# A four-layer kernel on one core: head 0's rows sent from the projection, wide exponentials in the last head, and identity products in layer 3's search

## The reference, cut to what matters

```python
# layer 0, attention: 16 heads of 8, all 2048 tokens
scores = norm * jnp.einsum('hbqk,hbnk->hbqn', Q, K)
attn = jax.nn.softmax(scores, axis=-1)
heads = jnp.einsum('hbqn,hbnv->hbqv', attn, V)
...
# layer 3, feed-forward: 8 experts, each takes its 256 best tokens of those left
for e in range(E):
    s = jnp.where(taken, -jnp.inf, scores[:, e])
    _, idx = jax.lax.top_k(s, C)
    parts.append(idx)
    taken = taken.at[idx].set(True)
...
h = jax.nn.gelu(jnp.einsum('ecd,edf->ecf', h, w1) + b1[:, None, :])
h = jnp.einsum('ecf,efd->ecd', h, w2) + b2[:, None, :]
```

## Time and profile before

| what | value |
|---|---|
| median of 3 runs | 1740.68 us |
| lowest and highest run | 1740.24 and 1742.91 us |
| the profiled execution, its own time | 1742.6 us |
| its span, first to last instruction | 1740.8 us |
| mean granted TensorE clock | 0.806 |
| TensorE, VectorE, ScalarE, GpSimd busy | 72, 75, 51, 14% of the span |

### The profile page before, as it was taken

One profiled execution on the slowest core, in us unless ns is written; L12 is line 12 of the kernel. 1 busy time (PEld: TensorE's weight loads), 2 busy tenths in 40 slices (PEclk: granted clock), 3 DMA queues, 4 the chain that ended last, 5 costly groups with the idle time before them and its releaser, 6 DMA issues. The chain is left out here.

```text
span 1740.8 us, 29844 instructions
## 1 busy us (share of the span) xinstructions
PE 1251.1 (72%) x10670; PEld 619.5 (36%) x10674; DVE 1303.1 (75%) x3511; ACT 894.3 (51%) x1789; POOL 237.7 (14%) x279
## 2 busy tenths in 40 slices
PE   6799999999999998475994463060205989833776
PEld 3122222222222223254983342040104556622444
DVE  4999999999999971537237336979898469568783
ACT  4089999999999998322421122020001675512453
POOL 3000000000000000003510314030001321100223
PEclk9589999999999999567995586565656898965668
DMA  2101100001100000000004331000001721022001
GB/s 66 43 3 27 29 21 21 20 23 28 28 22 21 20 3 2 15 29 1 1 1 174 109 84 48 0 0 1 1 1 26 209 69 47 16 93 70 22 22 31
DMA packets 45095, 62.88 MB, mean 36 GB/s; under 512 B 12849, under 2 KB 34420, under 8 KB 44548
## 3 DMA queue, kind: packets, MB, share of 16 engines
q1 hardware_dynamic: 38115, 49.45, 9.6%
q0 software_dynamic: 5568, 10.81, 2.5%
q10 hardware_dynamic: 1264, 0.72, 0.2%
HBM read 34.10 MB, written 13.63 MB: 27 GB/s over the span
## 5 line engine op out<-in xcount | busy, mean ns | idle before, releaser
L822 ACT ACTIVATE l0att_probs<-l0att_ps_sv 128x512 f32<-128x512 f32 x1024 | 555.7, 596 | 84.0 <-PE l0att_ps_sv L792 71.9
L859 DVE TENSOR_REDUCE l0att_half_negmax<-l0att_ps_m 128x1 f32<-128x1024 f32 x480 | 547.2, 1215 | 6.0 <-PE l0att_ps_m L731 6.0
L761 PE MATMUL l0att_ps_sv<-l0att_probs,l_V_aug 128*32 128x256 f32 x4096 | 331.1, 392 | 5.3 <-ACT l0att_pv_sb L813 5.3
L792 PE MATMUL l0att_ps_sv<-l_Q,l_K 51*128 51x512 bf16 x1024 | 200.7, 388 | 2.5 <-ACT l0att_probs L822 0.2
L731 PE MATMUL l0att_ps_m<-l_K,l_Q 48*128 48x512 bf16 x960 | 186.0, 385 | 11.1 <-DVE l0att_half_negmax L859 7.1
L761 PEld LDWEIGHTS l0att_ps_sv<-l0att_probs,l_V_aug 128*32 128x32 f32 x4096 | 83.2, 108 | 199.1 <-issue 104.4
L792 PEld LDWEIGHTS l0att_ps_sv<-l_Q,l_K 51*128 51x128 bf16 x1024 | 49.5, 92 | 216.7 <-ACT l0att_probs L822 204.1
L472 POOL CAST l0att_nm<-l0att_negmax 128x16 bf16<-128x16 f32 x16 | 3.1, 196 | 513.3 <-DVE l0att_negmax L835 513.3
L2826 ACT ACTIVATE l3loc_probs<-l3loc_ps_s 128x320 f32<-128x320 f32 x128 | 48.8, 435 | 37.3 <-PE l3loc_ps_s L2803 36.7
L2004 DVE SCALAR_TENSOR_TENSOR l2spk_lif_v<-l2spk_U 128x64 f32<-128x64 f32 (+1 forms) x368 | 60.4, 205 | 0.0
L2269 PE MATMUL l2spk_ps<-l_X,l2spk_w_terms 128*128 128x512 bf16 x48 | 13.0, 441 | 62.3 <-DVE l_X L2299 62.3
(11 more groups left out here) (734 smaller groups left out, 2358.0 us busy)
## 6 DMA issues: line engine op xcount, KB each, us to landing
l_Q<-l_qp SPq DMA_DIRECT2D x188, 32.0 KB
l_K<-l_kp SPq DMA_DIRECT2D x188, 32.0 KB
l1ffn_W<-in_l_expert_w_dram SPq DMA_DIRECT2D x1, 4096.0 KB
l3f_experts_l_w<-in_l_w_dram SPq DMA_DIRECT2D x2, 2048.0 KB
l_sorted_in<-l1ffn_zeros SPq DMA_DIRECT2D x1, 3072.0 KB
l1exp_rows<-l_sorted_in SPq DMA_DIRECT2D x6, 512.0 KB, 5.4
l_sorted_out<-l1exp_y SPq DMA_DIRECT2D x6, 512.0 KB
l_Q<-in_local_mask_q_dram POOLq DMA_DIRECT2D x2, 1170.0 KB, 18.8
```

The source lines that it names most:

```text
L761: mm = pe.matmul(ps_v[32 * c:32 * c + 32, cols], V_aug[:, kt, h, :], probs[:, kt % 2, c, cols], start=(kt == 0 and part == 0), stop=(kt == ...
L792: pe.matmul(ps_s[:, (n + i) % 3, :], K[at, h % HEAD_BUFS, c1(kt)], Q[at, h % HEAD_BUFS, c4(2 * pair + i)], start=True, stop=True).then_inc ...
L822: act.activation(probs[:, kt % 2, c, :], ps_s[:, n % 3, :], ACT.Exp).then_inc(expd, 1)
L859: dve.tensor_reduce(half_negmax[:, h % 2, t, half:half + 1], src, AX_X, ALU.max, negate=True).then_inc(m_read, 1)
```

## The change

1. The projection of layer 0 gets a callback. SyncE waits there for each part of K and then of Q and issues head 0's 12 low-half transfers as the parts come; the attention block no longer issues them, and TensorE there waits for one semaphore that they all raise.
2. In head 15 the scores of two banks are taken by one exponential of 1,024 columns. The first pair of a key tile goes into a half of `ps_m`, the second into the first two banks of `ps_sv`. Both parts of the value products stand behind the second pair; behind the first pair stands nothing.
3. In the search the digit is added to the result one round later, behind the sum and ahead of the candidates' step (in the half's last round also, with a wait), and for the last digit at the old place.
4. Behind the count and the beside work of rounds 1 to 7 TensorE multiplies the identity up to four times into `ps_t`: four times less two where places are due (rounds 2 to 5 from search 1 on), less two where an expert's up or down products are due (rounds 1 to 5 and 7 from search 2 on).

```diff
+                if rows_of_part is not None:
+                    for m, which in enumerate((1, 0)):
+                        read = NC4 * (m + 1)
+                        sp.wait_ge(high_read, read)
+                        rows_of_part(sp, which, 0)
+                        sp.wait_ge(middle_read, read)
+                        rows_of_part(sp, which, 1)
+                        for done in low_read:
+                            sp.wait_ge(done, read // 2)
+                        rows_of_part(sp, which, 2)
...
+        def first_rows(sp, which, part):
+            for r in range(6):
+                if (SPLITS_Q, SPLITS_K)[which][r] == part:
+                    load_piece(sp, Q, K, qp, kp, 0, loaded_first, 0, r, which)
...
             def _(sp):
-                for piece in low[0::3]:
-                    load_piece(sp, 0, loaded_first, *piece)
                 for piece in high:
...
             def _(pool):
-                for piece in low[2::3]:
-                    load_piece(pool, 0, loaded_first_pool, *piece)
...
-                pe.wait_ge(loaded_first, LOAD // 3)
-                pe.wait_ge(loaded_first_pool, LOAD // 6)
+                pe.wait_ge(loaded_first, LOAD // 2)
...
-                            if n >= 2:
+                            last = h == L0_H - 1
+                            if last and kt >= 1:
+                                pe.wait_ge(last_expd, 2 * kt + pair - 1)
+                            elif last and pair == 0:
+                                pe.wait_ge(m_read, place["nm", h] + 1)
+                            elif last:
+                                pe.wait_ge(expd, (L0_H - 1) * NT * NC4)
+                            elif n >= 2:
                                 pe.wait_ge(expd, n - 1)
...
+                            if last and pair == 0:
+                                continue
                             while todo and (pair == 1 or len(todo) > len(plan[h, kt]) // 2):
                                 run(todo.pop(0))
-                            if kt >= 1:
-                                values(h, kt - 1, pair)
-                            elif h >= 1:
-                                values(h - 1, NT - 1, pair)
+                            for part in range(2) if last else [pair]:
+                                if kt >= 1:
+                                    values(h, kt - 1, part)
+                                elif h >= 1:
+                                    values(h - 1, NT - 1, part)
...
             def _(act):
-                for piece in low[1::3]:
-                    load_piece(act, 0, loaded_first, *piece)
...
-                for n in range(L0_H * NT * NC4):
+                for n in range((L0_H - 1) * NT * NC4):
...
+                for n in range(2 * NT):
+                    kt, pair = n // 2, n % 2
+                    if n == 2:
+                        copy_values(L0_H - 2)
+                    for i in range(2):
+                        act.wait_ge(last_scored[i], n + 1)
+                    act.wait_ge(pv_done, (L0_H - 1) * NT + kt - 1)
+                    act.activation(probs[:, kt % 2, 2 * pair:2 * pair + 2, :].rearrange("p c n -> p (c n)"),
+                                   last_pair[pair], ACT.Exp).then_inc(last_expd, 1)
...
                         beside(k, i)
+                        if i >= 1:
+                            used = 2 * (k >= 1 and 2 <= i <= 5) + 2 * (k >= 2 and i <= 7 and i != 6)
+                            keep_busy(pe, g, ps_t, 4 - used)
...
                         smaller = step >> DIGIT
+                        if i >= 1:
+                            add_digit(step << DIGIT)
+                            if i + 1 == DIGITS:
+                                link.wait()
                         if i + 1 < DIGITS:
...
-                        link.mark(dve.scalar_tensor_tensor(result, digit[:], float(step), result, ALU.mult, ALU.add))
-                        if i + 1 < DIGITS:
+                        if i + 1 == DIGITS:
+                            add_digit(step)
+                        else:
                             link.mark(dve.scalar_tensor_tensor(cands[:, 0, :], bcast(digit[:], P, CAND), float(step),
                                                                cands[:, 0, :], ALU.mult, ALU.add))
```

More of the change, by code:

```diff
@@ L480, in rest_parts, with stage_project_parts @@
     eng.tensor_tensor(parts[2], rest, parts[1], ALU.subtract).then_inc(done, 1)
[L483 removed]
+def stage_project_parts(nc, loads, w_name, g, layer, name, V_aug, qp, kp, q=None, drams=(), stored=None, beside=None,
+                        rows_of_part=None):
     CHUNKS = 2 * NC4
@@ L598, in _, with load_piece, stage_l0_attend @@
                 pool.wait_ge(v_filled, 2)
-def stage_l0_attend(nc, loads, g, V_aug, qp, kp, Q, K, ones_placed, O):
+def load_piece(eng, Q, K, qp, kp, h, landed, half, r, which):
+    operand, parts, part = ((Q, qp, SPLITS_Q[r]), (K, kp, SPLITS_K[r]))[which]
+    at = HALF_ROWS * half + r
+    eng.dma_start(operand[at:at + TERMS - 5:6, h % HEAD_BUFS, :], parts[part][h:P:L0_H, :]).then_inc(landed, 16)
+def stage_l0_attend(nc, loads, g, V_aug, qp, kp, Q, K, ones_placed, loaded_first, O):
     LEAD = 4
@@ L3348, in search, with add_digit @@
                     link(dve.tensor_scalar(cands[:], multiples[:], float(step), lowest, ALU.mult, ALU.add))
+                    def add_digit(step):
+                        link.mark(dve.scalar_tensor_tensor(result, digit[:], float(step), result, ALU.mult, ALU.add))
                     for i in range(DIGITS):
```

31 lines of the change are left out of this document (15 added, 16 removed).

## The result

The changed kernel takes 1734.48 us, the median of six runs (1729.18 to 1737.56), beside 1742.53 for the kernel before: a ratio of 0.9948, 95% interval 0.9932 to 0.9964, so 6 to 12 us faster. The forecast was 1732, the range 1726.5 to 1737.5. The total came out near the forecast, its parts did not: two gains were larger, and the search, which was to get 1 to 4 us shorter, got 4.4 us longer.

A forecast was written before the change was run, and what follows sets the result against it. No engine bounds the whole; ScalarE bounds head 15, and a VectorE-TensorE ring makes the search round. Terms -4.1 - 3.0 - 2.2 + 0.2 = -9.1 us gave 1731.6 from the median 1740.68, forecast as 1732, range 1726.5 to 1737.5.

The forecast's parts named there:

- a search not 1 to 4 us shorter: Layer 3's search: a sign that the prediction is wrong, unless the search gets 1 to 4 us shorter.
- Head 0's rows: Start of layer 0's attention: rows sent from the projection let TensorE start near 38.6, minus 4.1 us (3.4 to 4.9 earlier).
- Wide exponentials: Head 15 of layer 0's attention: 32 exponentials for 64 save 0.10 each; counted minus 3.0 us, between 1.0 and 3.6.
- The digit: Search rounds: the addition moved under TensorE's turn saves 0.08 us in 27 rounds, minus 2.2 us.
- The products: Search: 88 identity products raise the clock but delay some counts, 3.6 us against 3.4, plus 0.2 us.
- of the 3.2 us of lateness I let 2.9 go: Seven searches: the raised clock removes 2.9 of the 3.2 us by which TensorE's counts come late.
- the cold starts: First searches before the clock rises: products delay three rounds each by about 0.1 us, 0.6 in all.
- The clock stays low behind the products: Search rounds 6 and 7: products at a low clock cost 16.5 us, whole plus 8, median 1749; chance 0.04.
- Its second price: Round 7 of the searches: a cold 1.8 us of products meets masks wanted some 1.2 after the count, 4.2 us.
- TensorE sets head 15's pace: Head 15: TensorE bounds the wide exponentials, so they gain 1.0 instead of 3.0 us, whole 1734; chance 0.15.
- Head 0's rows don't come sooner: Attention's start: the last transfer or the barrier waits, the rows' edit gives 0 to 1 us, whole 1735.5; chance 0.05.
- The clock helps in full: Searches and tail: the clock stays up over the borders, products give 3.5 us, whole near 1728; chance 0.16.

The follow-up runs named there:

- wide_only: The kernel before with head 15's exponentials of 1,024 columns alone: 1739.79 us, ratio 0.9971 to the kernel before.
- digit_only: The kernel before with the moved digit addition of the search alone: 1741.24 us, ratio 0.9981 to the kernel before.
- products_only: The kernel before with the 88 identity products alone: 1748.92 us, ratio 1.0032 to the kernel before.
- over_the_border: Changed kernel with two digit columns, products only from search 2 and not in round 6, four more at the border from search 3: 1732.76 us, ratio 0.9934.
- products_in_gap: Changed kernel with two digit columns and, for its products, only four in each of searches 2 to 6, around rounds 0 and 1: 1728.49 us, ratio 0.9919.
- two_digit_columns: The changed kernel without its products and with the digit kept in two columns by turns: 1729.43 us, ratio 0.9924 to the kernel before.
- no_products: The changed kernel without its 88 identity products: 1731.58 us, ratio 0.9922 to the kernel before.
- not_round6: The changed kernel with the products left out in round 6 of each search: 1732.26 us, ratio 0.9934 to the kernel before.
- round6_only: The changed kernel with its products in round 6 of each search alone: 1734.79 us, ratio 0.9958 to the kernel before.

## Why the prediction was right, and where it was not

The total lay near the forecast (-8.05 by the medians, -8.7 forecast from 1740.68 to 1732), but this is in part luck: two gains that came out 2.4 us larger hid a part of the 5.8 us by which digit and products came out worse. One of the signs that the prediction gave for being wrong, a search not 1 to 4 us shorter, did come.

**Head 0's rows** (-4.1 forecast, -5.7 measured, outside its end of -4.9). Mechanism and order were right, to the issue of the last transfer: at 35.55 forecast, and found there. The step that was mis-sized is "From issue to landing the shown transfers took 2.3 to 3.4, median 2.7": this one, issued 1.14 behind the one before it, took 1.91 until TensorE ran, and "TensorE starts some 0.3 later" was no cost of its own. That gives 1.1 of the 1.6; the rest, 0.42, is the clock, still 1.00 at 37.46, by which VectorE followed TensorE in 0.64 and not in 1.06.

**Wide exponentials** (-3.0, measured -3.8). The exponential forecast as 1.02 is 1.025, and the step forecast as 0.96 is 0.956 on average where the stage runs evenly (0.913, 0.920, 1.070, 0.920). The step that was mis-sized is the one before: "the step from start to start is (4.31 - 0.596) / 7 = 0.531". In the trace steps of 0.494 and 0.582 alternate, and those seven hold four short ones and three long ones; the mean is 0.538, which over 64 makes 0.45 us. So what goes with each exponential is 3.81 / 32 = 0.12 and not 0.10. The other part is the 0.3 taken off for TensorE: its 1.9 us a key tile was too much (it is busy for 28.00 / 16 = 1.75), and by the prediction's own terms two groups of values at 0.79 would make 2.4 and not the 2.1 of its lower end. The Trainium skill (ScalarE: Activation LUTs, Rules for kernel authors) budgets about 0.3 us for an activation whose bias is a [128,1] operand; by it the prediction estimated 9.6 us. These exponentials are given no such bias, so the 3.8 us of wide_only says what the figure is here and does not contradict that page.

**The digit** (-2.2, measured about -0.9). The undisturbed round went from 1.71 to 1.64 (from round 5's count to round 6's in search 4 of digit_only, 1665.65 to 1667.29), beside the 0.08 forecast. That "it is covered when VectorE waits for the count" failed for the last round of each half: the work was covered, but not the second wait on the comparison, 0.09 in most of these rounds and 0.44 once. Two columns gave back 1.02 with 0.32 more lateness, so 1.34, and 0.85 + 1.34 is the 2.2 of the forecast.

**The products** (+0.2, measured +4.7). What they take in round 7 was sized well: 2.1 + 0.9 forecast, 3.8 less 0.3 of before found. Two other steps failed. The first is "of the 3.2 us of lateness I let 2.9 go": by rounds, the lateness before stands in round 3 (1.8 us) and round 5 (1.0), and after it is 3.0 and 0.4. The products raised the mean clock, as forecast, to above 0.7 in searches 0 and 1, but by rounds 4 to 7, while it was 0.50 at 18 of the 21 counts of rounds 1 to 3 in all seven searches. A mean clock of a stretch was taken for a clock at the place of the wait. The second is the cold starts, forecast at 0.6 for the first searches. Rounds 2 and 3 went from 1.9 to 4.0 us late: 1.25 of it is in searches 0 and 1, and 0.9 in searches 2, 3 and 6.

Of the rivals, "The clock stays low behind the products" did not come: the clock was 1.00 at round 6's count in six of the kernel after's seven searches and 0.8 in the other. Its second price, masks behind round 7's products at the low clock, did come in one search of the kernel after (0.5 us), in three of products_only's and in three of over_the_border's. That the clock rose in search 0 behind nothing but counts and products (0.50 to 0.77) shows that plain products with the identity do raise it. The Trainium skill (TensorE: Matmul & The Clock Gate, Part 4: PE-mode transpose) says of transposes in that mode that they don't count as activity; no run here sets those apart. "TensorE sets head 15's pace" and "Head 0's rows don't come sooner" fell by the rows above. "The clock helps in full" has 1728, which none reached by a full clock: products_in_gap has 1728.49 with the rounds no shorter than without products (118.15 beside 118.22 in two_digit_columns).

So the sum came out at -5.7 - 3.8 - 0.9 + 4.7 = -5.7 by the traces, against -9.1; the medians have -8.05 with an interval of 6 to 12. The 2.3 us between the two are not explained: the stretches that no edit touches became 2.6 us shorter and the norm 2.7 longer in the profiled executions. That loss in the norm is of no edit's doing: of the 14 kernels nine have 13.6 to 13.9 there and five 16.1 to 16.4, with and without products. What decides whether the clock is at 0.50 there was not found; the products are not it, since no_products has 16.14 and not_round6 13.60, and they come later than that stretch.

## What to carry to other kernels

Filler work for the clock belongs on an in-order engine only where nothing that another engine waits for stands behind it: price it at the low clock, at each place, and look at the clock round by round at the places of the waits, not at its mean. In these searches TensorE's clock was low behind the stretches where it had little to do; filling one border kept it up there, and it fell at a later round instead. A second wait on an instruction of a tight ring costs even where that second one is long fulfilled; here another buffer took it away. And a change of several edits should be taken apart before it is believed: here by the ratios three of them brought 13.6 us (no_products, 0.9922), and the fourth gave 4.5 back.

## What the runs showed of the hardware

- The transfer of 32 KB that SyncE issued at 35.55, 1.14 us behind the one before it, was there for TensorE 1.91 us from its issue (run after). With twelve issued within 2.5 us on three queues, the one issued at 38.89 was followed by TensorE only at 42.77, 3.9 later; which of the twelve landed last the trace doesn't show.
- The comparison starts 0.23 behind the start of the count when it waits for the count alone (before, two_digit_columns), and 0.31 to 0.32 when it waits for its own engine too (digit_only; once 0.67).
- Products of the identity take 0.22 us a pass at clock 0.50 (the eight weight loads in round6_only, 1.78 us) and 0.12 at 1.00 (the eight weight loads of round 6 in search 4 of the kernel after, 0.97 us). So four products are 1.8 us at the low clock, longer than the 1.64 us of the round in which they stand.
- Exponentials from PSUM start 0.494 and 0.582 us apart by turns at 512 columns, and 0.92 apart at 1,024 where nothing holds them (head 15, before and after).
- Kernels that are alike in a stretch differ by 2.8 us in the norm and by 4.6 us in the tail. The granted clock differs with them: 0.50 against 0.63 or 0.75 in the norm; in the tail less closely, with 36.02 us at 0.93, but 38.06 and 40.71 both at 0.81.
